# Two int4 unpacking steps half a pair later, and a layer-1 sample in front of a weight fold

## The chip, the core and the metric

The kernel runs on one core of one Trainium2 chip. The metric is the device time in microseconds (us) of one execution; the times given are medians over several executions.

## The reference

x has 32 samples of 64 channels and 1024 positions. Two levels follow each other, each adding its result to x:

```python
x = x + _L0_ffn_ref(_L0_cond_ref(x, cond_512, ...), A, B, Wr)
x = x + _L1_ffn_ref(_L1_cond_ref(x, cond_512, ...), qweight, scales, zeros, bias)
# cond: four convolutions (same, upsample, same, downsample) of 3 taps, 64 to 64 channels,
#   whose weights are modulated per sample by a style vector and normalised
# ffn of level 0: a router takes 16 of 64 experts; h = xf A, out = (h * G) B
# ffn of level 1: an int4 matrix, 8 nibbles packed in an int32:
nib = qw[:, None, :] >> shifts[None, :, None] & jnp.uint32(15)
W = scales[:, 0][None, :] * q - zeros[:, 0][None, :]
out = jnp.einsum('bsi,io->bso', x, W) + bias
```

## The kernel before

The samples go in pairs. Level 0 has pairs c = 0 to 15, level 1 has pairs c = 16 to 31 (NPAIR = 16). Matrix products in float32 are made of three products of rounded parts: each operand is split in a high part (ScalarE writes it by an ACTIVATE) and a low part (VectorE subtracts), so most steps have the form "TensorE multiplies into PSUM, ScalarE writes hi, VectorE writes lo, TensorE multiplies". Every engine has its own instruction stream, written out by hand; an engine does its instructions in the order written, and semaphores hold one engine for another.

The steps of a pair, by function:
- split (L736 on ScalarE writes x_hi, L745 on VectorE writes x_lo) and layer1 on TensorE (six matmuls, L181 to L183, into conv_ps[a]); act_layer1 (L762, L764, L765) and dve_layer1 (L167) give h_hi and h_lo.
- The upsampling, same and downsampling convolutions are folded to one set of weights per sample: fold_start (v_hi, v_lo) -> fold3 (TensorE L666; r_hi L680; r_lo L685) -> fold2 (TensorE L701, fifteen matmuls; e_hi L713, L715, L716; e_lo L167, L725, L726).
- cond multiplies h by the folded weights (twelve matmuls per sample, L181 to L183) and act_cond (L785) copies the result to cond.
- From level 1's pair 16 on the ffn follows three pairs (AHEAD) behind: turn (L812 transposes, L818) and quant (L966, L967).

The matrix of the level-1 ffn is unpacked once, in eight steps k. dve_nibbles shifts and masks packed into one of two nibble buffers (L1081); act_nibbles casts it into quant (L1086). The first quant product waits for all eight. The samples' first and last positions are made separately for all samples of a level (the edges): plain_edge_vector (VectorE steps 0 to 4) and plain_edge_tensor (TensorE layers 0 to 3, L402) alternate, and the last step gives cond_edge, which the ends of every cond need (act_ends).

Between the loops over level 0 and over level 1 stand pairs 17, 18 and 19, written out; that is where the edges and the nibbles are placed between the steps of the pairs. Level 1 then runs in a loop over three pairs at a time.

Of the kernel before, what the change touches and what calls it, by code (L numbers as in the profile page):

```python
# [28 lines left out]
KT = D // P  # L29
# [11 lines left out]
def program(nc, t):  # L41
    with ExitStack() as outer:
# [31 lines left out]
        S = Buffers()  # L74
# [90 lines left out]
        def low(out, whole, hi):  # L165

            return nc.vector.tensor_tensor(out, whole, hi.bitcast(F32), ALU.subtract)  # L167
# [9 lines left out]
        def products(out, stationary, hi, lo, moving_hi, moving_lo):  # L177

            n = len(stationary)
            for i, w in enumerate(stationary):  # L180
                nc.tensor.matmul(out, hi(w), moving_hi(i), start=(i == 0), stop=False)  # L181
                nc.tensor.matmul(out, hi(w), moving_lo(i), start=False, stop=False)  # L182
                last = nc.tensor.matmul(out, lo(w), moving_hi(i), start=False, stop=(i == n - 1))  # L183
            return last

        def tiles(w):
            return lambda q: w[:, q, :]

        def windows(w):
            return lambda q: w[:, q * C:q * C + P]  # L190
# [500 lines left out]
        def pe_fold2(pe, c, bufs, first=False):  # L691
            pe.wait_ge(S.fold3_ready, 2 * c + 2)
            if first:
                pe.wait_ge(S.lo["f2"], bufs.first_sample // B + 1)
            if not first or bufs.first_sample:
                pe.wait_ge(S.fold2_hi, 2 * c)
                pe.wait_ge(S.fold2_ready, c)
            for n, (tile, m, block) in enumerate(FOLD2):
                out = fold_ps[1][:, block * P:(block + 2) * P]
                for i, (w, r) in enumerate(((fold2_hi, bufs.r_hi), (fold2_hi, bufs.r_lo), (fold2_lo, bufs.r_hi))):  # L700
                    last = nc.tensor.matmul(out, windows(w)(tile), r[:, m:R_PAIRS:2, :, :], start=(n == 0 and i == 0),  # L701
                                            stop=(n == len(FOLD2) - 1 and i == 2), skip_group_check=True)
            last.then_inc(S.fold2_done, 1)


        def act_fold2(act, c, bufs, first=False):
            act.wait_ge(S.fold2_done, c + 1)
            if not first or bufs.first_sample:
                act.wait_ge(S.cond_done, 2 * c)
            flat = lambda ap: ap.rearrange("p q a m -> p (q a) m")  # L710
            blocks = fold_ps[1][:, :].rearrange("p (q o) -> p q o", o=C)
            hi = bufs.e_hi
            nc.scalar.activation(flat(hi[:, :, :, 0:C]), blocks, ACT.Identity).then_inc(S.fold2_hi, 1)  # L713
            act.wait_ge(S.fold2_hi, 2 * c + 1)
            nc.scalar.activation(flat(hi[0:C, :, :, C:P]), flat(hi[C:P, :, :, 0:C]).bitcast(F32), ACT.Identity)  # L715
            nc.scalar.activation(flat(hi[C:P, 0:E_PAIRS - 1, :, C:P]), flat(hi[0:C, 1:E_PAIRS, :, 0:C]).bitcast(F32), ACT.Identity).then_inc(S.fold2_hi, 1)  # L716

        def dve_fold2(v, c, bufs):
            flat = lambda ap: ap.rearrange("p q a m -> p (q a) m")
            blocks = fold_ps[1][:, :].rearrange("p (q o) -> p q o", o=C)  # L720
            v.wait_ge(S.fold2_hi, 2 * c + 1)
            lo = bufs.e_lo
            low(flat(lo[:, :, :, 0:C]), blocks, flat(bufs.e_hi[:, :, :, 0:C])).then_inc(S.fold2_lo, 1)
            v.wait_ge(S.fold2_lo, c + 1)
            nc.vector.tensor_copy(flat(lo[0:C, :, :, C:P]), flat(lo[C:P, :, :, 0:C]).bitcast(F32))  # L725
            nc.vector.tensor_copy(flat(lo[C:P, 0:E_PAIRS - 1, :, C:P]), flat(lo[0:C, 1:E_PAIRS, :, 0:C]).bitcast(F32)).then_inc(S.fold2_ready, 1)  # L726
# [21 lines left out]
        def pe_layer1(pe, c, a, bufs, first=False):  # L748
            pe.wait_ge(S.xin_split, 2 * c + a + 1)
            if first:  # L750
                pe.wait_ge(S.lo["w1"], bufs.first_sample // B + 1)
            if not first or bufs.first_sample:
                pe.wait_ge(S.cond_out, 2 * c + a - 1)
            cut = lambda w: (lambda i: w[a][:, i:i + H])
            products(conv_ps[a][:, :], (0, 1), tiles(w1_hi), tiles(w1_lo), cut(bufs.x_hi), cut(bufs.x_lo)).then_inc(S.layer1_done, 1)


        def act_layer1(act, c, a, bufs):
            act.wait_ge(S.layer1_done, 2 * c + a + 1)
            act.nop(nofuse=True)  # L760
            ps, hi = conv_ps[a], bufs.h_hi[a]
            nc.scalar.activation(ps[:, :], ps[:, :], ACT.Identity, bias=at(bias1, c, a, bufs), scale=at(scale1, c, a, bufs)).then_inc(S.layer1_scaled, 1)  # L762
            act.wait_ge(S.layer1_scaled, 2 * c + a + 1)
            nc.scalar.activation(hi[0:C, 1:H + 1], ps[0:C, :], ACT.Identity)  # L764
            nc.scalar.activation(hi[C:P, 2:H + 2], ps[C:P, :], ACT.Identity).then_inc(S.layer1_hi, 1)  # L765

        def dve_layer1(v, c, a, bufs):
            v.wait_ge(S.layer1_hi, 2 * c + a + 1)
            low(bufs.h_lo[a][0:C, 1:H + 1], conv_ps[a][0:C, :], bufs.h_hi[a][0:C, 1:H + 1])
            low(bufs.h_lo[a][C:P, 2:H + 2], conv_ps[a][C:P, :], bufs.h_hi[a][C:P, 2:H + 2]).then_inc(S.layer1_ready, 1)  # L770
# [11 lines left out]
        def act_cond(act, c, a, bufs):  # L782
            act.wait_ge(S.cond_done, 2 * c + a + 1)
            act.nop(nofuse=True)
            nc.scalar.activation(bufs.cond[:, a, 1:H - 1], conv_ps[a][:, 1:H - 1], ACT.Identity, bias=at(bias4, c, a, bufs),  # L785
                                 scale=at(demod_tab[:, LAYERS - 1, :], c, a, bufs)).then_inc(S.cond_out, 1)
# [290 lines left out]
        def dve_nibbles(v, first, end):  # L1077
            for k in range(first, end):
                if k >= 2:
                    v.wait_ge(S.quant_ready, k - 1)  # L1080
                nc.vector.tensor_scalar(nibble[k % 2][:, :], packed[:, :], 4 * k, 15, ALU.logical_shift_right, ALU.bitwise_and).then_inc(S.nibble_ready, 1)  # L1081

        def act_nibbles(act, first, end):
            for k in range(first, end):
                act.wait_ge(S.nibble_ready, k + 1)
                nc.scalar.activation(quant[:, k, ONES:], nibble[k % 2][:, :], ACT.Identity).then_inc(S.quant_ready, 1)  # L1086
# [149 lines left out]
        def _(pe):  # L1236
# [73 lines left out]
            slot = lambda f: buf1[f % SLOTS]  # L1310
            f, c = NPAIR - 1, NPAIR
# [13 lines left out]
            c = NPAIR + 1  # L1325
# [6 lines left out]
            c = NPAIR + 2  # L1332
# [5 lines left out]
            for a in range(2):  # L1338
                pe_cond(pe, c, a, slot(c))
            i, c = NPAIR, NPAIR + AHEAD  # L1340
            pe_fold2(pe, c, slot(c))
            pe_layer1(pe, c, 0, slot(c))
            plain_edge_tensor(pe, 1, set1, 2)
            pe_layer1(pe, c, 1, slot(c))
            plain_edge_tensor(pe, 1, set1, 3)
# [47 lines left out]
        def _(act):  # L1393
# [78 lines left out]
            f, c = NPAIR - 2, NPAIR - 1  # L1472
# [17 lines left out]
            slot = lambda f: buf1[f % SLOTS]  # L1490
            f, c = NPAIR - 1, NPAIR
# [8 lines left out]
            c = NPAIR + 1  # L1500
# [10 lines left out]
            act_fold3(act, c + 1, slot(c + 1))  # L1511
            split(c + 1, slot(c + 1))
            act_cond(act, c, 0, slot(c))
            act.wait_ge(S.edges_copied, 1)
            act_nibbles(act, 6, KT)
            act_cond(act, c, 1, slot(c))
            c = NPAIR + 2
            act_fold_start(act, c + 1, slot(c + 1))
# [2 lines left out]
            act_layer1(act, c, 1, slot(c))  # L1521
            act_fold3(act, c + 1, slot(c + 1))
            split(c + 1, slot(c + 1))
            for a in range(2):
                act_cond(act, c, a, slot(c))
            c = NPAIR + AHEAD
            act_fold2(act, c, slot(c))
            act_layer1(act, c, 0, slot(c))
            act_layer1(act, c, 1, slot(c))
            act.wait_ge(S.edges_done, 2)  # L1530
            for f in range(NPAIR, NPAIR + AHEAD):
# [37 lines left out]
        def _(v):  # L1569
# [7 lines left out]
            def split(c, bufs, first=False):  # L1577
                for a in range(2):
                    dve_split(v, c, a, bufs, first)
# [77 lines left out]
            slot = lambda f: buf1[f % SLOTS]  # L1657
            f, c = NPAIR - 2, NPAIR - 1
# [15 lines left out]
            f, c = NPAIR - 1, NPAIR  # L1674
# [8 lines left out]
            c = NPAIR + 1  # L1683
# [16 lines left out]
            nc.vector.memset(set1.edge[1][0:C, 1, 2, :], 0.0)  # L1700
            nc.vector.memset(set1.edge[2][:, :, :, :], 0.0)
            plain_edge_vector(v, 1, set1, 0)
            dve_nibbles(v, 6, KT)
            c = NPAIR + 2
            dve_fold3(v, c, slot(c))
            split(c, slot(c))
# [5 lines left out]
            c = NPAIR + AHEAD  # L1712
            dve_fold3(v, c, slot(c))
            split(c, slot(c))
            plain_edge_vector(v, 1, set1, 2)
            dve_fold2(v, c, slot(c))
            plain_edge_vector(v, 1, set1, 3)
            dve_layer1(v, c, 0, slot(c))
            plain_edge_vector(v, 1, set1, 4)
            dve_layer1(v, c, 1, slot(c))  # L1720
            v.wait_ge(S.consts_loaded, 16 * 3)
# [99 lines left out]
```

## Time and profile before

| | |
|---|---|
| median of 3 runs | 923.52 us (923.03 to 924.61) |
| profiled execution | 923.16 us, span 921.5 us |
| TensorE (PE) busy | 910.3 us, 99% of the span |
| VectorE (DVE) busy | 489.0 us, 53% |
| ScalarE (ACT) busy | 408.5 us, 44% |
| GpSimd (POOL) busy | 89.6 us, 10% |

The span runs from the first to the last instruction of the profiled execution; times within it are counted from its start. The pairs that the change touches are in the stretch from about 617 to 650 us. In a timeline an engine's idle time before an instruction stands in brackets, with what ended it. The ends of matmuls are modelled, and one starts before the one ahead of it has ended, so gaps on TensorE are better read from start to start.

### The profile page before, as it was taken

How to read it: one execution, taken by the hardware profiler on the slowest of the kernel's cores; microseconds unless marked ns; L12 is line 12 of the kernel's file. 1: busy time of each engine (PE TensorE's matmuls, PEld its weight loads, DVE VectorE, ACT ScalarE, POOL GpSimd, SP SyncE). 2: the span in 40 equal slices, each digit the busy share in tenths (PEclk: the TensorE clock that was granted, in tenths of full speed). 3: DMA queues.
4: the chain of work that ended last, by engine and by line, in shares of the span. 5: the costliest groups of instructions: out<-in, count | busy, mean ns of one | idle time of the engine just before them, and what ended most of it. 6: DMA issues, size and time to landing. Idle time of an engine off the chain costs nothing.

```text
span 921.5 us, 14606 instructions
## 1 busy us (share of the span) xinstructions
PE 910.3 (99%) x5012; PEld 823.1 (89%) x5012; DVE 489.0 (53%) x1069; ACT 408.5 (44%) x762; POOL 89.6 (10%) x113
## 2 busy tenths in 40 slices
PE   7999999999999999999999999999999999999998
PEld 6889889899899899898898998988998999999998
DVE  7885434344345245254343355587666556666555
ACT  5943423423333244243234234387555565655540
POOL 0000000000000000000000030311211121111121
PEclk9999999999999999999999999999999999999999
DMA  8801201201102112012012011333222222122111
GB/s 289 274 10 60 68 23 46 67 11 59 46 23 68 31 37 68 23 46 68 23 46 68 18 63 47 63 99 131 69 76 86 91 91 68 68 76 84 69 69 69
DMA packets 33132, 64.29 MB, mean 70 GB/s; under 512 B 11728, under 2 KB 14032, under 8 KB 33104
## 3 DMA queue, kind: packets, MB, share of 16 engines
q1 hardware_dynamic: 24032, 30.90, 11.6%
q0 software_dynamic: 9072, 33.03, 9.9%
q8 instruction: 16, 0.26, 0.1%
q14 instruction: 12, 0.10, 0.0%
HBM read 47.14 MB, written 16.78 MB: 69 GB/s over the span
## 4 chain that ended last, share of the span: by engine, by line
PE 94%; DVE 3%; ACT 1%; issue 0%; DMA 0%; DVEq 0%; ACTq 0%
PE conv_ps L181 9%; PE conv_ps L183 9%; PE conv_ps L182 9%; PE prod_ps L891 6%; PE fold_ps L701 6%; PE prod_ps L892 6%; PE prod_ps L893 6%; PE prod_ps L858 5%; PE prod_ps L860 5%; PE prod_ps L859 5%; PE prod_ps L967 4%; PE prod_ps L966 4%; PE fold_ps L666 3%; PE turn_ps L812 3%; PE turn_ps L860 2%; PE turn_ps L858 2%
## 5 line engine op out<-in xcount | busy, mean ns | idle before, releaser
L181 PE MATMUL conv_ps<-h_hi,e_hi 128*128 128x512 f32 x256 | 102.9, 402 | 1.2 <-DVE h_lo L167 1.1
L167 DVE TENSOR_TENSOR h_lo<-conv_ps,h_hi 64x512 fp32r<-64x512 f32 x128 | 88.1, 688 | 29.9 <-ACT h_hi L765 28.6
L183 PE MATMUL conv_ps<-h_hi,e_lo 128*128 128x512 f32 x256 | 101.3, 396 | 0.0
L182 PE MATMUL conv_ps<-h_lo,e_hi 128*128 128x512 f32 x256 | 101.2, 395 | 0.0
L785 ACT ACTIVATE cond<-conv_ps,bias,demod_tab 128x510 f32<-128x510 f32 x64 | 49.8, 779 | 103.4 <-PE conv_ps L183 103.4
L891 PE MATMUL prod_ps<-b_hi,xt 128*128 128x512 f32 x240 | 93.5, 389 | 0.0
L892 PE MATMUL prod_ps<-b_lo,xt 128*128 128x512 f32 x240 | 93.4, 389 | 0.0
L893 PE MATMUL prod_ps<-b_hi,xt 128*128 128x512 f32 x240 | 93.4, 389 | 0.0
L858 PE MATMUL prod_ps<-a_hi,xt 128*128 128x384 f32 x240 | 81.1, 338 | 0.0
L860 PE MATMUL prod_ps<-a_hi,xt 128*128 128x384 f32 x240 | 81.1, 338 | 0.0
L859 PE MATMUL prod_ps<-a_lo,xt 128*128 128x384 f32 x240 | 81.0, 338 | 0.0
L966 PE MATMUL prod_ps<-quant,xt_hi 128*128 128x342 f32 x256 | 80.7, 319 | 0.0
L967 PE MATMUL prod_ps<-quant,xt_lo 128*128 128x342 f32 x256 | 80.6, 320 | 0.0
L818 ACT ACTIVATE xt<-turn_ps 128x512 fp32r<-128x512 f32 x32 | 17.4, 595 | 142.3 <-PE turn_ps L812 142.2
L903 ACT ACTIVATE xt<-turn_ps 128x512 fp32r<-128x512 f32 x32 | 17.4, 595 | 136.2 <-PE turn_ps L867 136.2
L167 DVE TENSOR_TENSOR xt<-turn_ps,xt 128x512 fp32r<-128x512 f32 x64 | 41.2, 686 | 66.4 <-ACT xt L903 48.3
L745 DVE SCALAR_TENSOR_TENSOR x_lo<-x_in,style_tab,x_hi 128x513 fp32r<-128x513 f32 x64 | 45.8, 757 | 56.1 <-ACT x_hi L736 56.1
L951 DVE SCALAR_TENSOR_TENSOR res<-prod_ps,norm,res 128x512 f32<-128x512 f32 x32 | 24.0, 751 | 94.3 <-PE prod_ps L893 92.1
L181 PEld LDWEIGHTS conv_ps<-h_hi,e_hi 128*128 128x128 f32 x256 | 48.3, 189 | 11.5 <-issue 1.5
L183 PEld LDWEIGHTS conv_ps<-h_hi,e_lo 128*128 128x128 f32 x256 | 48.3, 188 | 11.2
L182 PEld LDWEIGHTS conv_ps<-h_lo,e_hi 128*128 128x128 f32 x256 | 48.4, 189 | 9.3
L181 PE MATMUL conv_ps<-x_hi,w_hi 128*128 128x512 f32 x128 | 53.9, 421 | 0.0
(269 smaller groups left out, 2108.3 us busy)
## 6 DMA issues: line engine op xcount, KB each, us to landing
x_in<-in_x SPq DMA_DIRECT2D x64, 128.0 KB, 2.8
res<-in_x POOLq DMA_DIRECT2D x16, 512.0 KB, 3.6
x_after_first<-res POOLq DMA_DIRECT2D x16, 512.0 KB, 2.9
x_in<-x_after_first SPq DMA_DIRECT2D x64, 128.0 KB, 2.7
res<-x_after_first POOLq DMA_DIRECT2D x16, 512.0 KB, 3.6
out_x<-res POOLq DMA_DIRECT2D x15, 512.0 KB, 2.9
a_raw<-in_adapter_in SPq DMA_DIRECT2D x8, 544.0 KB, 8.3
b_raw<-in_adapter_out SPq DMA_DIRECT2D x8, 512.0 KB, 11.6
```

The costliest lines, as they stand in the source:

```text
L167: return nc.vector.tensor_tensor(out, whole, hi.bitcast(F32), ALU.subtract)
L181: nc.tensor.matmul(out, hi(w), moving_hi(i), start=(i == 0), stop=False)
L182: nc.tensor.matmul(out, hi(w), moving_lo(i), start=False, stop=False)
L183: last = nc.tensor.matmul(out, lo(w), moving_hi(i), start=False, stop=(i == n - 1))
L858: nc.tensor.matmul(out, bufs.xt_hi[:, k, :], bufs.a_hi[:, k, cols], start=(k == 0), stop=False)
L859: nc.tensor.matmul(out, bufs.xt_hi[:, k, :], bufs.a_lo[:, k, cols], start=False, stop=False)
L860: last = nc.tensor.matmul(out, bufs.xt_lo[:, k, :], bufs.a_hi[:, k, cols], start=False, stop=(k == KT - 1))
L891: nc.tensor.matmul(prod_ps[n][:, :], bufs.xt_hi[:, k, :], bufs.b_hi[:, k, cols], start=(k == 0), stop=False)
L892: nc.tensor.matmul(prod_ps[n][:, :], bufs.xt_hi[:, k, :], bufs.b_lo[:, k, cols], start=False, stop=False)
L893: last = nc.tensor.matmul(prod_ps[n][:, :], bufs.xt_lo[:, k, :], bufs.b_hi[:, k, cols], start=False, stop=(k == KT - 1))
L966: nc.tensor.matmul(out, bufs.xt_hi[:, k, :], bufs.quant[:, k, cols], start=(k == 0), stop=False)
L967: last = nc.tensor.matmul(out, bufs.xt_lo[:, k, :], bufs.quant[:, k, cols], start=False, stop=(k == KT - 1))
```

## The change

The last two unpacking steps (k = 6, 7) move. On ScalarE they stood between cond of (17,0) and cond of (17,1), and now stand between cond of (18,0) and cond of (18,1), with the wait for the copied edges. On VectorE they stood after edge step 0, ahead of fold3 of pair 18, and now stand after the split of pair 19, ahead of edge step 2. In pair 19 (the fourth of level 1) layer 1 of sample 0 goes in front of fold2 on all three engines. On VectorE edge step 3 keeps its place behind fold2, and h_lo of (19,0), which stood behind edge step 3, is now ahead of both.

```diff
@@ TensorE
             i, c = NPAIR, NPAIR + AHEAD
+            pe_layer1(pe, c, 0, slot(c))
             pe_fold2(pe, c, slot(c))
-            pe_layer1(pe, c, 0, slot(c))
             plain_edge_tensor(pe, 1, set1, 2)
             pe_layer1(pe, c, 1, slot(c))
             plain_edge_tensor(pe, 1, set1, 3)
@@ ScalarE
             act_cond(act, c, 0, slot(c))
-            act.wait_ge(S.edges_copied, 1)
-            act_nibbles(act, 6, KT)
             act_cond(act, c, 1, slot(c))
             c = NPAIR + 2
             act_fold_start(act, c + 1, slot(c + 1))
...
             act_fold3(act, c + 1, slot(c + 1))
             split(c + 1, slot(c + 1))
-            for a in range(2):
-                act_cond(act, c, a, slot(c))
+            act_cond(act, c, 0, slot(c))
+            act.wait_ge(S.edges_copied, 1)
+            act_nibbles(act, 6, KT)
+            act_cond(act, c, 1, slot(c))
             c = NPAIR + AHEAD
+            act_layer1(act, c, 0, slot(c))
             act_fold2(act, c, slot(c))
-            act_layer1(act, c, 0, slot(c))
             act_layer1(act, c, 1, slot(c))
@@ VectorE
             plain_edge_vector(v, 1, set1, 0)
-            dve_nibbles(v, 6, KT)
             c = NPAIR + 2
             dve_fold3(v, c, slot(c))
             split(c, slot(c))
...
             c = NPAIR + AHEAD
             dve_fold3(v, c, slot(c))
             split(c, slot(c))
+            dve_nibbles(v, 6, KT)
             plain_edge_vector(v, 1, set1, 2)
+            dve_layer1(v, c, 0, slot(c))
             dve_fold2(v, c, slot(c))
             plain_edge_vector(v, 1, set1, 3)
-            dve_layer1(v, c, 0, slot(c))
             plain_edge_vector(v, 1, set1, 4)
             dve_layer1(v, c, 1, slot(c))
```

## Rows read from the trace of the kernel before

**Rows 1.** The page, its first lines: busy us (share of span) xinstructions.
```profile
span 921.5 us, 14606 instructions
PE 910.3 (99%) x5012; PEld 823.1 (89%) x5012; DVE 489.0 (53%) x1069; ACT 408.5 (44%) x762; POOL 89.6 (10%) x113
```
**Rows 2.** Waits of PE, whole span: us in total, times, longest.
```profile
PE conv_ps L181 <- DVE h_lo L167: 1.1, 2, 0.6
PE turn_ps L867 <- DVE cond L937: 1.0, 1, 1.0
```
**Rows 3.** The chain that ended last, ahead of fold2 of pair 18: start us, us, engine.
```profile
619.10 1.29 DVE nibble L1081 x2
620.42 0.89 DVE r_lo L685 x2
```
**Rows 4.** Timeline of PE: start us, us, engine, line, operation, [idle before <-releaser].
```profile
620.23 0.26 PE L181 MATMUL prod_ps<-L_side_hi,w_hi 128*128 128x192 f32 x1
...
620.76 0.27 PE L183 MATMUL prod_ps<-L_side_hi,w_lo 128*128 128x192 f32 x1
621.35 0.39 PE L701 MATMUL fold_ps<-r_hi,fold_hi 128*128 128x256 f32 x1 [0.32 <-DVE r_lo L685]
...
627.75 0.34 PE L666 MATMUL fold_ps<-v_hi,fold_lo 128*128 128x384 f32 x1
628.62 0.50 PE L181 MATMUL conv_ps<-h_hi,e_hi 128*128 128x512 f32 x1 [0.53 <-DVE h_lo L167]
...
634.37 0.28 PE L701 MATMUL fold_ps<-r_hi,fold_hi 128*128 128x256 f32 x1
...
636.08 0.39 PE L181 MATMUL conv_ps<-x_hi,w_hi 128*128 128x512 f32 x1
...
637.47 0.81 PE L402 MATMUL prod_ps<-L_side,L_w_raw 128*128 128x192 f32 x4
637.98 0.53 PE L181 MATMUL conv_ps<-x_hi,w_hi 128*128 128x512 f32 x1
...
639.51 1.42 PE L402 MATMUL prod_ps<-L_side,L_down_flat 128*128 128x32 f32 x12
641.51 0.47 PE L181 MATMUL conv_ps<-h_hi,e_hi 128*128 128x512 f32 x1 [0.58 <-DVE h_lo L167]
```
**Rows 5.** Timeline of DVE, its rows around both places of the nibbles and edge step 3.
```profile
632.68 0.48 DVE L461 TENSOR_TENSOR L_side_turned<-prod_ps,scale 128x128 f32<-128x128 f32 x2
...
634.66 0.19 DVE L469 TENSOR_TENSOR L_side<-L_side,L_edge 64x32 f32<-64x32 f32 x1
636.91 0.69 DVE L167 TENSOR_TENSOR e_lo<-fold_ps,e_hi 128x512 fp32r<-128x512 f32 x1 [2.07 <-ACT e_hi L713]
...
638.46 0.36 DVE L472 SCALAR_TENSOR_TENSOR L_side_scaled<-prod_ps,scale 128x192 f32<-128x192 f32 x1
638.85 0.36 DVE L473 TENSOR_TENSOR L_side<-L_side_scaled,L_bias 128x192 f32<-128x192 f32 x1
639.97 1.39 DVE L167 TENSOR_TENSOR h_lo<-conv_ps,h_hi 64x512 fp32r<-64x512 f32 x2 [0.77 <-ACT h_hi L765]
```
**Rows 6.** Timeline of ACT, its rows at the casts, the conds and layer 1.
```profile
619.88 2.01 ACT L1086 ACTIVATE quant<-nibble 128x1024 fp32r<-128x1024 int32 x2 [1.28 <-DVE nibble L1081]
621.79 0.76 ACT L785 ACTIVATE cond<-conv_ps,bias,demod_tab 128x510 f32<-128x510 f32 x1
622.46 0.79 ACT L647 ACTIVATE v_hi<-down_T,scale 128x192 fp32r<-128x192 f32 x2
...
636.28 0.60 ACT L713 ACTIVATE e_hi<-fold_ps 128x512 fp32r<-128x512 f32 x1 [0.88 <-PE fold_ps L701]
...
637.98 0.72 ACT L762 ACTIVATE conv_ps<-conv_ps,bias,scale 128x512 f32<-128x512 f32 x1
...
639.34 0.59 ACT L765 ACTIVATE h_hi<-conv_ps 64x512 fp32r<-64x512 f32 x1
```
**Rows 7.** Timeline of PE at the head: two of six such matmuls.
```profile
12.20 0.63 PE L181 MATMUL conv_ps<-x_hi,w_hi 128*128 128x512 f32 x1
12.62 0.63 PE L182 MATMUL conv_ps<-x_lo,w_hi 128*128 128x512 f32 x1
```
**Rows 8.** Tile x_in from 615 to 660 us.
```profile
DMA to landing us min/median/max: 2.6/2.8/6.0
```

## The prediction

> **What bounds the kernel.** I read the page first, then who TensorE waited for, then the chain of work that ended last, then the timelines of TensorE, VectorE and ScalarE from 617 to 645 us. The page says that TensorE is busy for 910.3 us of a span of 921.5 [rows 1]: the time is TensorE's own work plus its few stalls. The list of waits shows how few they are after the head: the largest after the head are h_lo, twice, for 1.1 us together, and one of 1.0 us that lies before the edited stretch [rows 2]. The chain that ended last stays on TensorE nearly everywhere, except around the two edited pairs, where it leaves for the nibbles and r_lo of VectorE [rows 3]. After cond of sample (19,0) begins at 641.51 TensorE never stalls again for long, so whatever that start moves by should reach the end one for one. The question is therefore one number: when does cond(19,0) start?
>
> I write (c,a) for sample a of pair c. The timeline of TensorE [rows 4] holds three stalls; I count them from start to start, because a matmul overlaps the next:
> - fold2 of pair 18 starts at 621.35. The six matmuls of edge layer 0 before it start from 620.23 to 620.76, 0.11 apart, so it could start at 620.87: 0.48 lost, to r_lo.
> - cond(18,0) starts at 628.62; fold3 before it has its last start at 627.75 and a pitch of about 0.17, so 0.69 is lost, to h_lo of (18,0).
> - cond(19,0) starts at 641.51; edge layer 3 before it starts at 639.51 and lasts 1.42. After such a group the next matmul starts some 0.24 to 0.30 before its modelled end (637.47 + 0.81 = 638.28 against 637.98), so about 640.69: 0.82 lost, to h_lo of (19,0).
> Together 1.99 us. That is all that any reordering here can win.
>
> **Part one, the nibbles leave pair 17.** On VectorE two tensor_scalars of 1.29 us together start at 619.10, and r_lo, two operations of 0.89 together, follows at 620.42 [rows 3]. Without them r_lo can start at 619.10 (its input r_hi was ready at 616.7) and end at 619.98, so fold2 of 18 starts when TensorE is free, at 620.87 instead of 621.35: 0.48 gained. On ScalarE the two casts of 2.01 us in front of cond(17,1) go [rows 6]; its matmuls end at about 620.39, so it moves from 621.79 to 620.49, and ScalarE is idle again when fold2 ends.
>
> From there the order is fold2, e_hi, layer 1 of both samples on ScalarE, h_lo, cond(18,0). Each step starts from the one before, so all move by 0.48: the 0.69 stall stays as it is, and cond(18,0) starts at 628.14. e_lo of pair 18 is ready before 625.2, as VectorE is free at about 623.4. The edge steps 0 and 1 have more slack than they need. cond(18,1) ends so that TensorE is free at 634.37 - 0.48 = 633.89.
>
> SyncE issues the loads of pair 19 when x_lo of 18 is done, now near 621.5 instead of 622.8; the slowest landing in the stretch took 6.0 us [rows 8], and ScalarE wants the first at 629.38. This is hidden. The wait on the copied edges before the casts is over since 615.4 and costs nothing in either place.
>
> **Part two, where the nibbles land.** VectorE with the gain of 0.48 ends x_lo of 19 at about 632.2 (its next instruction started at 632.68 [rows 5]). Now the nibbles come: 632.20, first ready 632.89. ScalarE has meanwhile finished cond(18,0) at 632.1 and waits for them; the casts run from 632.98 for 2.01 us, and what is queued behind them is cond(18,1), which could have gone at 634.15 and now starts at 634.89 (0.10 of overlap, as before). Behind it stands layer 1 of (19,0), at 634.89 + 0.67 (the pitch from such a cond to the next instruction [rows 6]) + 0.02 = 635.58.
> VectorE goes on with edge step 2, 2.17 us (632.68 to 634.85 [rows 5]) from 633.5 to 635.67, while TensorE wants it only at 636.99. Hidden, with 1.3 us to spare.
>
> **Part three, the swap in pair 19.** TensorE does layer 1 of (19,0) (1.39 us from 633.89), fold2 (1.71, to 636.99), edge layer 2 (0.51, to 637.50), layer 1 of (19,1) (1.53, to 639.03); the pitches are differences of starts in [rows 4]. The instructions are the same, so nothing is paid for the swap on TensorE itself. None of these waits: layer 1 of (19,1) wants cond(18,1) copied out, which is at 635.67.
> Then comes edge layer 3. It needs edge step 3 of VectorE, and that is now queued behind h_lo of (19,0) and e_lo:
> - ScalarE layer 1 of (19,0): 635.58 + 1.95 (637.98 to 639.93 [rows 6]) = 637.53.
> - VectorE h_lo: from 637.56, two halves 1.39 [rows 5], to 638.95. e_hi comes from ScalarE (0.60 [rows 6]) at 638.18, so e_lo follows at once.
> - e_lo with its two copies: 636.91 to 638.46 is 1.55, so to 640.48.
> - edge step 3: 0.39 + 0.36, to 641.23.
> - TensorE starts 0.15 after that, as it did after h_lo (639.97 + 1.39 = 641.36 against 641.51), at 641.38.
> TensorE is thus idle from 639.03 to 641.38, 2.35 us, where before it had been served by 639.21 and did not wait. In the old order step 3 stood ahead of h_lo, and only fold2 in front of it. Edge layer 3 to the next start is 1.18 us (1.42 less 0.24), so cond(19,0) starts at 642.56. Its h_lo and e_lo are ready by 640.48, so the old stall of 0.82 is indeed gone; but a longer one stands one group earlier.
> **Sum:** 642.56 - 641.51 = +1.05 us. By stalls: -0.48 (fold2) - 0.82 (cond) + 2.35 (edge layer 3) = +1.05, the same.
>
> What follows has slack. Edge step 4 ends near 643.4, the ends of cond are written by 644.1, and the transposes want them at 645.4. h_lo of (19,1) is ready near 644.8, wanted at 646.3. GpSimd's first bias addition starts near 643.5 instead of 642.05, wanted at 653.
>
> The profiled execution took 923.16 us with a span of 921.5; the sum makes it 924.2. The median of the runs shown is 923.52, so I forecast 923.52 + 1.05 = 924.6, or 0.11% more. A measurement of this kernel can tell about 0.2% (1.85 us) from no change.
>
> **Bounds.** The gain at fold2 lies between 0 (something else holds it) and 0.48; with 0 the whole chain is later and the sum +1.53. The delay from VectorE to TensorE is 0.05 (r_lo ends at 621.30, fold2 at 621.35) to 0.15: 0.1 less. Some twelve overlaps of a few hundredths make perhaps 0.3 either way, an estimate. That gives +0.6 to +1.6, or 924.1 to 925.1.
>
> **Rivals.**
> 1. *The stall does not form at edge layer 3*, because the casts or layer 1 of (19,0) come through 1 us or more earlier than I added up. If VectorE's step 3 is done by 640, only part of the stall is left; if there is none, -0.48 - 0.82 = -1.30, or 922.2. Against it: VectorE's queue order forces h_lo and e_lo (2.9 us) between layer 1 and step 3. Even then the gain is under 0.2%; all three stalls gone would be -1.99, 921.5, and nothing touches the 0.69 one. Chance 0.13, from -1.3 to +0.4.
> 2. *The gain of pair 18 is not had*: r_lo early is worth nothing if another wait, x_lo or the loads crowding 617 to 627 us, takes its place. +1.53, 925.05. Chance 0.12.
> 3. *The clock falls in the new gap* (slower). TensorE at the head ran 512 columns with starts 0.42 us apart [rows 7], its lower level (1.2 GHz), against 0.23 at 2.4 GHz; it stayed there through 13.05 us and had begun after an idle 3.92. If a gap of 2.35 us, and behind it twelve matmuls of 32 columns, brought that level back, cond(19,0) alone would cost 12 x 0.19 = 2.3 us, and a lower level as long as at the head (9 us at half speed) 4.5. With the 1.05 this is +3.4 to +5.6, 926.9 to 929.1. It decides from the point where the gap is long enough; no stall after 15 us shows a fall, the longest being 1.0 [rows 2]. The Trainium skill ("TensorE: Matmul & The Clock Gate", Part 1) says that half rate is the default and activity releases it, so idleness can bring it back; no row here shows that happen. Chance 0.07.
> My forecast has 0.68.
>
> **Range.** The likeliest alone: 924.1 to 925.1. To leave out no more than 2 in 10 it takes in rival 2 and part of rival 1: 923.2 to 925.8. Faster by over 0.2% needs practically all stalls gone: 0.02. Slower by over 0.2% is rival 3 and a little of the upper tail: 0.10. Within: 0.88.
>
> **What would show it.** r_lo of 18 near 619.1, fold2 near 620.87 with no wait; cond(18,0) still waiting for h_lo; casts near 633.0; cond(18,1) on ScalarE near 634.9; a wait of edge layer 3 (L402) for VectorE's L473 of around 2 us ending near 641.4; cond(19,0) near 642.6 without a wait; all starts after that some 1.05 later. I would be wrong if L402 didn't wait, if matmuls after it started 0.42 apart, or if something past 645 us waits anew.

## The result and the profile after

The changed kernel takes 927.30 us (median of 19 executions, 924.12 to 929.11) against 923.33 (19 executions, 923.03 to 924.64): ratio 1.0035, 95% interval 1.0029 to 1.0041. It is 0.35% slower (the medians alone differ by 3.97 us or 0.43%), where 0.11% had been forecast. The profiled execution took 927.3 us with a span of 925.6, and its mean granted clock is 0.996 instead of 1.000. One execution of the experiments below (edge step 3 first; 993.57 us at a mean clock of 0.852) was in the chip's slow state and is left out of that run's range; without it that run's median would be 924.40.

The page of the changed kernel, its first lines (busy us, share of the span, instructions), to be read against [rows 1]:

```profile
span 925.6 us, 14606 instructions
PE 913.2 (99%) x5012; PEld 825.2 (89%) x5012; DVE 489.4 (53%) x1069; ACT 408.2 (44%) x762; POOL 89.5 (10%) x113
```

The instructions are as many, yet TensorE is busy for 2.9 us more. A mere wait would not add busy time: the same matmuls took longer. The waits of TensorE, against [rows 2]:

```profile
PE prod_ps L402 <- DVE L_side L473: 2.3, 1, 2.3
PE turn_ps L867 <- DVE cond L937: 1.0, 1, 1.0
...
PE conv_ps L181 <- DVE h_lo L167: 0.5, 1, 0.5
```

There is one new wait, the one forecast: edge layer 3 (L402) for VectorE's edge step 3 (L473). TensorE's timeline shows it and what came behind it (start, length, in brackets idle time and releaser; the rows of before are [rows 4]):

```profile
620.13 0.26 PE L181 MATMUL prod_ps<-L_side_hi,w_hi 128*128 128x192 f32 x1
...
620.78 0.31 PE L701 MATMUL fold_ps<-r_hi,fold_hi 128*128 128x256 f32 x1
...
627.94 0.47 PE L181 MATMUL conv_ps<-h_hi,e_hi 128*128 128x512 f32 x1 [0.54 <-DVE h_lo L167]
...
638.54 0.40 PE L183 MATMUL conv_ps<-x_hi,w_lo 128*128 128x512 f32 x1
641.22 2.06 PE L402 MATMUL prod_ps<-L_side,L_down_flat 128*128 128x32 f32 x12 [2.28 <-DVE L_side L473]
643.08 0.77 PE L181 MATMUL conv_ps<-h_hi,e_hi 128*128 128x512 f32 x1
643.66 0.63 PE L182 MATMUL conv_ps<-h_lo,e_hi 128*128 128x512 f32 x1
644.08 0.63 PE L183 MATMUL conv_ps<-h_hi,e_lo 128*128 128x512 f32 x1
...
648.35 1.33 PE L812 MATMUL turn_ps<-ident,cond 128*128 128x128 f32 x8
649.43 0.48 PE L181 MATMUL conv_ps<-h_hi,e_hi 128*128 128x512 f32 x1
649.75 0.39 PE L182 MATMUL conv_ps<-h_lo,e_hi 128*128 128x512 f32 x1
...
652.30 0.31 PE L966 MATMUL prod_ps<-quant,xt_hi 128*128 128x342 f32 x1
```

fold2 of pair 18 starts at 620.78 without a wait, as forecast. Behind the idle 2.28 us the matmuls of cond(19,0) start 0.42 to 0.43 apart and last 0.63, as those of the head did [rows 7]; from 649.75 they are 0.39 long again. The stretches of 2 us (columns: stretch, busy us of PE, PEld, DVE, ACT, POOL, then the granted clock, DMA share, GB/s) give the clock itself:

```profile
640.00:642.00 2.00, 0.78 (x7) 0.79 (x8) 1.08 (x4) 1.07 (x2) 0.00 (x0) 1.00 0.00 0
642.00:644.00 2.00, 2.00 (x9) 1.89 (x9) 0.66 (x3) 0.14 (x2) 0.04 (x1) 0.51 0.00 0
...
646.00:648.00 2.00, 2.00 (x6) 1.52 (x6) 0.00 (x0) 0.00 (x0) 2.00 (x2) 0.50 0.00 0
648.00:650.00 2.00, 2.00 (x13) 1.71 (x12) 0.07 (x1) 0.77 (x2) 0.68 (x1) 0.79 0.00 0
```

The clock is whole up to 642 us and half (1.2 of 2.4 GHz) from there to about 649. VectorE and ScalarE, at the step that makes TensorE wait, are where the sum had them (against [rows 5, 6]). First VectorE:

```profile
632.09 1.29 DVE L1081 TENSOR_SCALAR nibble<-packed 128x1024 int32<-128x1024 int32 x2
...
637.44 1.39 DVE L167 TENSOR_TENSOR h_lo<-conv_ps,h_hi 64x512 fp32r<-64x512 f32 x2 [1.98 <-ACT h_hi L765]
...
640.80 0.36 DVE L473 TENSOR_TENSOR L_side<-L_side_scaled,L_bias 128x192 f32<-128x192 f32 x1
```

and ScalarE, with one thing that the sum had not:

```profile
629.49 0.73 ACT L736 ACTIVATE x_hi<-x_in,style_tab 128x513 fp32r<-128x513 f32 x1 [0.20 <-DMA x_in<-x_after_first]
630.56 0.73 ACT L736 ACTIVATE x_hi<-x_in,style_tab 128x513 fp32r<-128x513 f32 x1 [0.34 <-DMA x_in<-x_after_first]
...
632.87 2.01 ACT L1086 ACTIVATE quant<-nibble 128x1024 fp32r<-128x1024 int32 x2 [0.91 <-DVE nibble L1081]
634.78 0.76 ACT L785 ACTIVATE cond<-conv_ps,bias,demod_tab 128x510 f32<-128x510 f32 x1
635.44 0.74 ACT L762 ACTIVATE conv_ps<-conv_ps,bias,scale 128x512 f32<-128x512 f32 x1
```

x_hi of pair 19 now waits for its loads, which it did not before.

**The bill.** The head differs by some tenths between executions, so I count from the start of edge layer 0 (620.13 here, 620.23 in [rows 4]). Up to cond(19,0) it is 22.95 us here and 21.28 before, +1.67. Of this, 0.50 is the lower clock already: from the start of edge layer 3 to cond(19,0) is 1.86 here and 1.36 where the clock held (the swap alone, below). The order of the engines thus costs 1.17. From cond(19,0) to the first quant product is 9.22 against 648.14 - 641.51 = 6.63, +2.59, all clock: TensorE has the same matmuls there and waits in neither. The row of before that this rests on:

```profile
648.14 0.31 PE L966 MATMUL prod_ps<-quant,xt_hi 128*128 128x342 f32 x1
```

Clock 3.09, order 1.17, together 4.26, less 0.10 for the earlier head: 4.16, and the spans differ by 4.1.

The 19 executions say the same by their mean granted clock. Two show 1.000 and took 924.12 and 924.46; five show 0.998, 925.65 to 926.29; eleven 0.996, 927.25 to 927.84; one 0.994, 929.11. Where the clock held, the time is the one forecast (924.1 to 925.1).

### The profile page after: what moved, and what is told of

The parts are those of the page before. It is cut to its first block, busy times and chain, and to the rows that moved or that the text cites. A ratio compares the mean times of both kernels' runs of the same rounds, so it can differ in the third digit from the quotient of the medians.

```text
span 925.6 us, 14606 instructions
## 1 busy us (share of the span) xinstructions
PE 913.2 (99%) x5012; PEld 825.2 (89%) x5012; DVE 489.4 (53%) x1069; ACT 408.2 (44%) x762; POOL 89.5 (10%) x113
## 4 chain that ended last, share of the span: by engine, by line
PE 94%; DVE 3%; ACT 1%; issue 0%; DMA 0%; DVEq 0%; ACTq 0%
PE conv_ps L181 9%; PE conv_ps L183 9%; PE conv_ps L182 9%; PE prod_ps L891 6%; PE prod_ps L892 6%; PE prod_ps L893 6%; PE fold_ps L701 6%; PE prod_ps L858 5%; PE prod_ps L860 5%; PE prod_ps L859 5%; PE prod_ps L967 4%; PE prod_ps L966 4%; PE fold_ps L666 3%; PE turn_ps L812 3%; PE turn_ps L858 2%; PE turn_ps L860 2%
## 5 line engine op out<-in xcount | busy, mean ns | idle before, releaser
L167 DVE TENSOR_TENSOR xt_lo<-turn_ps,xt_hi 128x512 fp32r<-128x512 f32 x32 | 20.6, 686 | 64.6 <-ACT xt_hi L818 64.6
```

## The experiments

All are compared with the kernel before on the same chip; its median was 923.24, 923.23 and 923.10 in the three sets. "From edge 0" is the time in the profile from the start of edge layer 0 to that of cond(19,0), 21.28 before and 22.95 in the change.

| run | from edge 0 | median us (range) | ratio, 95% interval |
|---|---|---|---|
| nibbles only | 21.04 | 923.30 (922.44 to 924.71) | 0.9998 (0.9989 to 1.0007) |
| swap only | 22.95 | 927.41 (926.27 to 927.82) | 1.0042 (1.0029 to 1.0056) |
| gap filled | 22.67 | 924.63 (924.03 to 926.77) | 1.0018 (1.0009 to 1.0027) |
| edge step 3 first | 21.16 | 924.50 (923.00 to 925.08) | 1.0009 (1.0000 to 1.0019) |
| half filled | 22.43 | 924.97 (924.25 to 927.81) | 1.0020 (1.0011 to 1.0029) |
| nibbles only, loads first | 20.64 | 922.59 (922.40 to 923.15) | 0.9993 (0.9984 to 1.0002) |
| best order | 20.20 | 923.85 (923.49 to 925.38) | 1.0008 (0.9999 to 1.0017) |
| best order, loads first | 20.21 | 923.66 (923.50 to 925.31) | 1.0006 (0.9997 to 1.0015) |
| the same, nibbles before edge step 4 | 20.21 | 922.07 (921.89 to 922.25) | 0.9988 (0.9979 to 0.9997) |
| gap filled, loads first | 22.36 | 924.27 (924.05 to 926.02) | 1.0013 (1.0004 to 1.0022) |

Each run has eleven executions, the swap alone five. Where the interval holds 1, the medians alone don't tell the run from the kernel before; what such a run says is then read from its trace.

**Nibbles only.** The change without its lines in pair 19:

```diff
             i, c = NPAIR, NPAIR + AHEAD
-            pe_layer1(pe, c, 0, slot(c))
             pe_fold2(pe, c, slot(c))
+            pe_layer1(pe, c, 0, slot(c))
...
+            act_fold2(act, c, slot(c))
             act_layer1(act, c, 0, slot(c))
-            act_fold2(act, c, slot(c))
...
-            dve_layer1(v, c, 0, slot(c))
             dve_fold2(v, c, slot(c))
             plain_edge_vector(v, 1, set1, 3)
+            dve_layer1(v, c, 0, slot(c))
```

> The nibbles move as in the change, and pair 19 keeps the order of before (fold2 ahead of layer 1 of sample 0). Theory G (a gap ahead of edge layer 3 made by VectorE's order, and a clock that falls because of that gap): without the swap VectorE's edge step 3 is done before TensorE asks, so no gap, no fall. fold2 of 18 is 0.5 earlier; cond of (18,1) on ScalarE is at 634.8, TensorE's layer 1 of (19,0) ends at 636.7, cond(19,0) starts near 640.8 instead of 641.5: 922.6 to 922.9, with all executions close together. Theory N (the nibbles in front of cond of (18,1) are what costs): 925 or more.

No gap ahead of edge layer 3 and no fall of the clock behind it; the nibbles are not what costs. The expected 922.6 to 922.9 or better was had by only five of the eleven executions (the median is 923.30), so part of the gain went elsewhere. The profiled one (923.57) shows two places. Edge layer 0 starts 0.58 later than before (620.81 against 620.23), and that is ahead of everything that was edited. From there on only 0.24 is gained, where some 0.7 was expected. ScalarE's timeline says why:

```profile
631.10 1.34 ACT L736 ACTIVATE x_hi<-x_in,style_tab 128x513 fp32r<-128x513 f32 x2 [1.14 <-DMA x_in<-x_after_first]
```

**Swap only.** The kernel before with just the lines in pair 19.

```diff
             i, c = NPAIR, NPAIR + AHEAD
+            pe_layer1(pe, c, 0, slot(c))
             pe_fold2(pe, c, slot(c))
-            pe_layer1(pe, c, 0, slot(c))
...
+            act_layer1(act, c, 0, slot(c))
             act_fold2(act, c, slot(c))
-            act_layer1(act, c, 0, slot(c))
...
+            dve_layer1(v, c, 0, slot(c))
             dve_fold2(v, c, slot(c))
             plain_edge_vector(v, 1, set1, 3)
-            dve_layer1(v, c, 0, slot(c))
```

> Pair 19 in the order of the change, the nibbles where they were before. Theory G: layer 1 of (19,0) ends on TensorE near 635.9, ScalarE and VectorE go on at once, step 3 stands behind h_lo and e_lo until about 641.6, TensorE waits from 639.5 for about 2.2 us, and the clock falls behind it as in the change: 926 to 928. Theory N: without the casts in front of cond of (18,1) the wait is short and the time is 923 to 924.

In the medians the swap alone is the whole loss. Its TensorE timeline and, below, its stretches:

```profile
33.73 1.09 PE L812 MATMUL turn_ps<-ident,cond 128*128 128x128 f32 x8 [0.40 <-ACT cond L791]
...
642.85 1.52 PE L402 MATMUL prod_ps<-L_side,L_down_flat 128*128 128x32 f32 x12 [2.13 <-DVE L_side L473]
644.21 0.48 PE L181 MATMUL conv_ps<-h_hi,e_hi 128*128 128x512 f32 x1
```

```profile
642.00:644.00 2.00, 1.15 (x11) 1.16 (x11) 0.72 (x3) 0.78 (x2) 0.00 (x0) 1.00 0.00 0
644.00:646.00 2.00, 2.00 (x10) 1.65 (x10) 1.54 (x4) 0.68 (x6) 0.94 (x1) 0.82 0.00 0
646.00:648.00 2.00, 2.00 (x6) 1.61 (x5) 0.22 (x1) 0.00 (x0) 2.00 (x2) 0.50 0.01 4
648.00:650.00 2.00, 2.00 (x12) 1.66 (x12) 0.00 (x1) 0.70 (x2) 1.76 (x1) 0.83 0.00 0
```

The idle 2.13 us end at 642.85, and the clock is still whole when cond(19,0) starts; it falls only after 645, when TensorE is dense again. So the fall follows the gap, but not at once, and when it comes differs between executions (the change's was at 642).

The 4.2 us by which this span is longer are made up otherwise than in the change. The order costs 1.67 up to cond(19,0), all at the whole clock, because the gain at fold2 of pair 18 is not had. The lower clock costs 1.54: from cond(19,0) to the first quant product (652.38) it is 8.17 against 6.63. The other 1.03 came ahead of edge layer 0 (621.26 against 620.23), and no edit touches that stretch; some 0.8 of it follows a late x_in: ScalarE waited 0.49 and 0.29 us for it near 28 us, and TensorE 0.40 for cond at 33.73, where before neither waited. So the 22.95 here and in the change agree by chance; the change's holds 0.50 of lower clock.

**Gap filled.** The change, with matmuls that nobody reads between layer 1 of (19,1) and edge layer 3:

```diff
             pe_layer1(pe, c, 1, slot(c))
+            for _ in range(19):
+                nc.tensor.matmul(turn_ps[0][:, 0:2 * P], w1_hi[:, 0, :], flat2(w1_hi), start=True, stop=True)
             plain_edge_tensor(pe, 1, set1, 3)
```

> The change, with 19 matmuls of 256 columns that nobody reads put in TensorE's gap ahead of edge layer 3 (about 2.2 of its 2.45 us). All real work starts when it can, as in the change. Theory G: edge layer 3 still starts at 641.2 but at the full clock, cond(19,0) near 642.4, and the time is what the gap alone costs: 923.3 + 1.05 = 924.4, with little spread between executions. A rival (the 3 us beyond the gap come from something else: the order of PSUM banks, late ends of cond, the loads): still 927.3.

TensorE's timeline, and one of its stretches:

```profile
638.97 2.44 PE L1346 MATMUL turn_ps<-w_hi 128*128 128x256 f32 x19
641.65 1.53 PE L402 MATMUL prod_ps<-L_side,L_down_flat 128*128 128x32 f32 x12 [0.24 <-DVE L_side L473]
643.01 0.48 PE L181 MATMUL conv_ps<-h_hi,e_hi 128*128 128x512 f32 x1
```

```profile
642.00:644.00 2.00, 2.00 (x15) 1.85 (x15) 0.75 (x3) 0.24 (x3) 0.14 (x1) 1.00 0.00 0
```

Edge layer 3 is as late as in the change (0.22 later, counted from edge layer 0), TensorE has more work, the clock is whole, and the kernel is 2.7 us faster. That is the experiment that settles the cause: idleness of TensorE, by way of its clock, costs those 2.7 us, and what the order costs by itself is left, 924.63 - 923.24 = 1.4. Eight executions lie between 924.03 and 924.79; three lie at 926.1 to 926.8.

**Edge step 3 first.** On VectorE:

```diff
             plain_edge_vector(v, 1, set1, 2)
+            plain_edge_vector(v, 1, set1, 3)
             dve_layer1(v, c, 0, slot(c))
             dve_fold2(v, c, slot(c))
-            plain_edge_vector(v, 1, set1, 3)
```

> The change, but on VectorE edge step 3 stands directly behind edge step 2, ahead of h_lo of (19,0). Theory G: step 3 runs at 637.6 to 638.3, edge layer 3 follows layer 1 of (19,1) without a wait at 638.8; h_lo then ends near 639.7 and e_lo near 641.2, so TensorE's wait, 1.3 us, stands ahead of cond(19,0) at 641.3. That is 0.2 us less than before and no long gap: 923.1 to 923.5. Were the length of all stalls together what matters to the clock, it would still fall: 926 or more.

The wait moved as expected; it stands ahead of cond(19,0) now, and its length is in the bracket:

```profile
639.08 1.42 PE L402 MATMUL prod_ps<-L_side,L_down_flat 128*128 128x32 f32 x12
641.60 0.47 PE L181 MATMUL conv_ps<-h_hi,e_hi 128*128 128x512 f32 x1 [1.09 <-issue]
```

Four executions took 923.00 to 923.25, as expected, and six 924.3 to 925.1, at a mean clock of 0.997 to 0.998. The range of the expectation held only the former. In the profiled one (923.25) the clock held, so where it fell in the six isn't shown; a wait of 1.1 us may be enough at times. None of the kernel before's 27 executions of that set was below 0.999.

**Half filled.** As the gap filled, with 9 matmuls instead of 19.

> The change with 9 unread matmuls of 256 columns at the start of the gap, so that TensorE is busy for about 1.1 us of it and idle for about 1.3 at its end. Theory G (gap 1.05, clock the rest): the idle stretch is about as long as the wait of 1.1 us in the run with edge step 3 first, where some executions kept the full clock and others did not. So between the two: 924.4 where the clock holds, at most 926 where it falls, median 924.4 to 925.5. A rival, in which the clock's fall is set by how late edge layer 3 is and not by idleness: 927, as the change.

924.97, of the expected size. Edge layer 3 still waited 1.21 us. Six executions took 924.25 to 924.97 at a clock of 1.000; the other five show 0.998 or 0.996 and 925.74 to 927.81. The profiled one (925.90) is one of these five, but its clock is whole from 620 to 652 us; it fell at the head (the last experiment shows how).

**Nibbles only, loads first.** On SyncE:

```diff
+            sp.wait_ge(S.xin_split, 2 * NPAIR + 6)
+            sp_load(sp, NPAIR + 3, False)
             for dst, src in ((scales, t["L1_ffn_scales"]), (zeros, t["L1_ffn_zeros"]), (bias, t["L1_ffn_bias"])):
                 sp.dma_start(dst[:, :], src.broadcast_to([P, D])).then_inc(S.consts_loaded, 16)
-            with sp.Fori(NPAIR + 2, END - 1) as i:
+            with sp.Fori(NPAIR + 3, END - 1) as i:
```

> The nibbles moved, pair 19 in the old order, and on SyncE the loads of pair 19 issued ahead of those of scales, zeros and bias. Theory L (the gain at fold2 of 18 is given back where x_in of pair 19 lands late, behind those loads and GpSimd's): x_hi of 19 follows r_hi without a wait, cond(19,0) starts 0.5 to 0.7 earlier than before, 922.5 in nearly all executions. A rival, that the residual loads of GpSimd are what crowds them: x_hi still waits and the time stays near 923.3. Should SyncE's constants arrive too late instead, GpSimd's first bias addition would be late and show as a wait of VectorE.

Theory L holds. The landings of x_in from 615 to 634 us in this run, to be read against [rows 8]:

```profile
DMA to landing us min/median/max: 2.5/3.0/3.5
```

In the change the same view shows

```profile
DMA to landing us min/median/max: 2.6/6.7/7.2
```

The loads of pair 19 are issued 1.3 us earlier in the change (621.51 instead of 622.81) and gain next to nothing by it, because they stand behind the three constants (1.5 MB). With them in front, all eleven executions lie within 0.75 us, and in the profiled one cond(19,0) starts 0.64 earlier than before, as expected.

**Best order, and with loads first.** From the change, TensorE puts edge layer 2 between layer 1 and fold2; the nibbles go late:

```diff
@@ TensorE
             pe_layer1(pe, c, 0, slot(c))
+            plain_edge_tensor(pe, 1, set1, 2)
             pe_fold2(pe, c, slot(c))
-            plain_edge_tensor(pe, 1, set1, 2)
@@ VectorE
-            dve_nibbles(v, 6, KT)
             plain_edge_vector(v, 1, set1, 2)
+            plain_edge_vector(v, 1, set1, 3)
             dve_layer1(v, c, 0, slot(c))
             dve_fold2(v, c, slot(c))
-            plain_edge_vector(v, 1, set1, 3)
             plain_edge_vector(v, 1, set1, 4)
+            dve_nibbles(v, 6, KT)
@@ ScalarE
             act_cond(act, c, 0, slot(c))
-            act.wait_ge(S.edges_copied, 1)
-            act_nibbles(act, 6, KT)
             act_cond(act, c, 1, slot(c))
...
                     act_ends(act, f, a, slot(f))
+            act.wait_ge(S.edges_copied, 1)
+            act_nibbles(act, 6, KT)
             act_turn(act, NPAIR, slot(NPAIR))
```

> An order that keeps what is good in the change: pair 19's layer 1 of sample 0 first, edge layer 2 behind it and ahead of fold2 on TensorE; VectorE does edge steps 2 and 3 before h_lo of (19,0); the nibbles go behind edge step 4 on VectorE and behind the ends of cond on ScalarE. ScalarE's cond of (18,1) is at 634.1 and nothing stands in front of h_hi of (19,0), done near 637.3; e_lo is ready near 640.3, cond(19,0) starts near 640.4 against 641.51 before, with a wait of 0.5. Quant is complete near 643.5, wanted at 647. 922.2, clock held; with a late landing of x_in of 19 it gives back up to 1 us of it.

> The order of the run before this one, with the loads of pair 19 ahead of scales, zeros and bias. Theory L: the late landings are gone, 922.1, all executions within 0.5 us. If the crowding is GpSimd's alone it is as the run before.

cond(19,0) starts at 20.2 from edge layer 0, 1.07 earlier than before, as worked out; yet both medians are some half a microsecond above before, and the 922.1 to 922.2 of both expectations was missed. A new stall of 1.3 us stood ahead of cond(19,1), here in the second of the two:

```profile
645.62 0.50 PE L181 MATMUL conv_ps<-h_hi,e_hi 128*128 128x512 f32 x1 [1.28 <-DVE h_lo L167]
```

VectorE's timeline shows its cause, and GpSimd's, below, its neighbour:

```profile
640.77 3.50 DVE L1081 TENSOR_SCALAR nibble<-packed 128x1024 int32<-128x1024 int32 x2
644.19 1.39 DVE L167 TENSOR_TENSOR h_lo<-conv_ps,h_hi 64x512 fp32r<-64x512 f32 x2
```

```profile
641.00 5.49 POOL L1210 TENSOR_TENSOR res<-res,bias 128x1024 f32<-128x1024 f32 x2 [22.03 <-DVE cond_edge L477]
```

The longer of the two nibble operations took 2.89 us, against 0.69 for the median of all eight. Theory L is right about the landings here too (2.9 us in the median), but they were not what this order lacked.

**Nibbles before edge step 4.** The run before, with one swap on VectorE:

```diff
+            dve_nibbles(v, 6, KT)
             plain_edge_vector(v, 1, set1, 4)
-            dve_nibbles(v, 6, KT)
             dve_layer1(v, c, 1, slot(c))
```

> The run before (best order, loads of pair 19 first) with the nibbles on VectorE ahead of edge step 4 instead of behind it. Theory P: the two nibble operations took 3.50 us there instead of 1.29 because they ran beside GpSimd's first bias addition, which edge step 4 releases; ahead of step 4 they take 1.29 again, h_lo of (19,1) ends near 643.5, before TensorE wants it at 644.1, and the 1.28 us stall ahead of cond(19,1) goes: 922.1 to 922.3, clock held in all executions. A rival, that they are slow because of their place (the matmuls or ScalarE beside them): 3.5 us again and 923.6.

```profile
640.36 1.30 DVE L1081 TENSOR_SCALAR nibble<-packed 128x1024 int32<-128x1024 int32 x2
...
641.99 1.39 DVE L167 TENSOR_TENSOR h_lo<-conv_ps,h_hi 64x512 fp32r<-64x512 f32 x2
```

1.30 us again, the stall is gone, and all eleven executions lie between 921.89 and 922.25, as expected: 0.12% faster than before (interval 0.03% to 0.21%) and some 5 us faster than the change. GpSimd's additions start at 642.21 in this run, beside h_lo, whose 1.39 us are what it takes alone.

**Gap filled, loads first.**

> The change with its gap filled by 19 unread matmuls and the loads of pair 19 ahead of the constants. This takes away the two things that scatter the change's time, the clock's fall and the late landing; what is left is the order of the engines alone, which the sum put at +1.05: 924.2 in all executions, within 0.3. If the executions still scatter up to 926.5, as 3 of 11 did with the gap filled alone, the late landing was not their cause.

Eight executions took 924.05 to 924.56, which is the sum of the prediction. Three still took 925.8 to 926.0, so the late landing did not cause that scatter, and this part of the expectation fell. The profiled execution is one of the three, and shows what did; TensorE's timeline at the head:

```profile
12.09 0.40 PE L182 MATMUL conv_ps<-x_lo,w_hi 128*128 128x512 f32 x1
12.32 0.40 PE L183 MATMUL conv_ps<-x_hi,w_lo 128*128 128x512 f32 x1
14.68 0.69 PE L666 MATMUL fold_ps<-v_hi,fold_hi 128*128 128x384 f32 x1 [1.96 <-DVE v_lo L652]
```

```profile
10.00:14.00 4.00, 2.72 (x12) 2.02 (x10) 3.65 (x13) 1.78 (x5) 0.00 (x0) 1.00 0.87 286
14.00:18.00 4.00, 3.32 (x10) 3.06 (x10) 2.16 (x7) 2.93 (x7) 0.00 (x0) 0.58 0.98 376
18.00:22.00 4.00, 4.00 (x22) 3.13 (x22) 3.58 (x10) 2.49 (x5) 0.00 (x0) 0.99 1.03 420
```

Here the matmuls of the first layer ran at the whole clock early (0.23 apart), so TensorE came to fold3 sooner, waited 1.96 us for v_lo, and had the half clock behind it (0.58 in the mean from 14 to 18 us). Edge layer 0 starts at 621.93 in this execution, 1.7 later than before. The profiled executions of the half-filled run and of the best order show the same (waits of 2.0 and 1.9, edge layer 0 at 621.84 and 621.74). It is the kernel's own head, which all versions share. That it befalls the others too is likely and not shown: of the 81 executions of the kernel before in the three sets, five have a mean clock of 0.998 and took 924.52 to 924.85, and none of them has a profile.

## Why the prediction was wrong, step by step

- *The gain at fold2 of pair 18, 0.48.* Right: from edge layer 0 to fold2 is 0.65 in the change, 1.12 before.
- *The stall of cond(18,0) stays.* Right: idle 0.54 against 0.53.
- *The casts delay cond(18,1), and layer 1 of (19,0) with it.* Right: 634.78 and 635.44, forecast 634.89 and 635.58 (0.10 of it is the head).
- *The gap ahead of edge layer 3.* Right: forecast to end at 641.38 after 2.35 us, measured 641.22 with 2.28 idle in the bracket (2.45 from start to start, as the forecast counts). The working has a slip of 0.02: 638.95 + 1.55 is 640.50.
- *The sum, +1.05.* Right in size: 1.17 in the profile. The missing 0.12 is edge layer 3, which takes 1.36 to the next start and not 1.18 when it begins from rest, less 0.06 by which the gap ended earlier (counted from edge layer 0). With the gap filled and the loads in front the median is 924.27, or +1.17 on that set's 923.10. The two executions of the change with the clock whole took 924.1 and 924.5.
- *Rival 3, the clock falls in the new gap, chance 0.07.* This is the step that failed, and it was the likeliest case: the sum takes all of TensorE's work behind the gap at the whole clock, and 17 of the 19 executions have a mean clock of 0.998 or less. I argued that "no stall after 15 us shows a fall, the longest being 1.0". Those rows say nothing of a stall of 2.35, more than twice as long, and a small chance did not follow from them. The rival's price was right, in the lower half of its range: +3.4 to +5.6 forecast, 4.0 in the medians, 4.26 in the profile; the lower clock lasted beyond cond(19,0) and cost 3.09. The Trainium skill ("TensorE: Matmul & The Clock Gate", Part 1) has half rate as the default that activity lifts. The trace agrees: 0.51 and 0.50 behind the gap, and 1.00 again from 649 us, after TensorE had worked on without a wait.
- *"This is hidden", of the loads of pair 19.* Wrong as a statement, of no weight in the change: x_hi waited 0.20 and 0.34 for them. The landing time of 6.0 us was read as if it came with the load, while it is set by what is in the queues at that time; issued 1.3 us earlier, it took 7.2. Without the swap it cost 0.40 in the profiled executions (21.04 against 20.64 from edge layer 0) and 0.7 in the medians, 923.30 against 922.59, which hold the scatter of the head too.
- *Rival 1* did not come; the wait was there in full. *Rival 2* neither.

The likeliest range and the stated one, up to 925.8, left the fall out; the upper end ought to have gone to rival 3.

What stays open: executions of about 1.5 us more at a mean clock of 1.000 (two with the gap filled, one each with the nibbles only, the swap only (926.27), the best order with loads first, and of the kernel before (924.60)). The late x_in near 28 us, which the profiled runs with the nibbles only and the swap only show, came with 0.6 and 0.8 us at a whole clock and may be part of it. Open as well: why the clock of two executions of the change held and that of one fell for longer, and where it fell in those executions of the run with edge step 3 first that were not profiled.

## What to carry to other kernels

A new wait of an engine that was hardly ever idle can cost more than its length: TensorE paid 1.17 us for the late order and 3.09 us for the clock that fell behind it. When a reordering gives TensorE a gap longer than any in the trace, the longest gap seen is no evidence that the clock will hold; price the fall as a case of its own, and fill the gap or spread it. Check mean clock and spread over the executions too: one version here lies within 0.4 us in all its executions (922.07) and the change scatters over 5 us, in groups that go with the mean clock. But look at the whole trace before you blame the edit: a second source of scatter, at the kernel's head, was there all along.

Before a step is moved on one engine, list what stands behind it in that engine's queue and who is waiting there: edge step 3 kept its place in the list and was still made 2 us late by h_lo moving in front of it.

## What the runs showed of the hardware

- 2.1 to 2.3 us of idle TensorE in the middle of the kernel, and 1.96 at its head, were followed by the half clock for some 3 to 7 us. It began by 642 us in the change, where edge layer 3 started at 641.22, and some 2.4 us after that start in the swap alone (642.85, the first long matmul at 645.22). Waits of 1.0 to 1.3 us did no such thing in any profiled execution; six that were not profiled, with a wait of 1.1 us in their order, had a mean clock of 0.997 to 0.998.
- VectorE's shift-and-mask of 128x1024 int32 takes 0.69 us and took up to 2.89 us while GpSimd added two tensors of 128x1024; moved ahead of that it took 0.69 us again. GpSimd's own two additions took 5.49 us instead of 4.76. The Trainium skill ("SBUF — State Buffer", Who interferes with whom) says that the two engines share a pair of ports, that a tensor_scalar can use both pairs of VectorE's, and that the one that comes second waits for the whole instruction of the first. The trace agrees: the 2.89 us are the operation's own 0.69 and 2.20 more, most of one addition of GpSimd (4.76 / 2 = 2.38). The operation ended at 644.27, about its own 0.69 behind the end of GpSimd's first addition (641.00 + 2.7).
- The granted clock of the profile reads 1.00 at the head of the kernel before too, where matmuls of 512 columns start 0.42 us apart [rows 7]: the records begin with a whole clock that TensorE doesn't have yet. The mean clock of an execution leaves that part out: 9 us at half rate would make it 0.995, and it reads 1.000.
